# Linear attention of the second layer: weighted sums with the values stationary, denominators by running sums

## The chip, the cores and the metric

The kernel runs on one core of a Trainium2 chip. Its time is the device time of one execution in microseconds (us). TensorE (PE) multiplies, VectorE (DVE), ScalarE (ACT) and GpSimd (POOL) compute, SyncE (SP) only issues transfers. Every engine works through its own instructions in program order and waits on semaphores. Matrix products land in eight PSUM banks of 512 float32 columns; POOL cannot read them.

## The reference

Four layers follow each other on an input of 8 batches of 512 positions and 128 channels. Each layer adds an attention and a feed-forward part to its input. Only the attention of the second layer changes:

```
q = phi((x @ W_Q.T).reshape(b, t, H, DK))      # phi(u) = elu(u) + 1, H = 8 heads, DK = 64
k = phi((x @ W_K.T).reshape(b, t, H, DK))
v = (x @ W_V.T).reshape(b, t, H, DK)
gamma = sigmoid(decay_log)                     # one decay for each head
S = gamma * S + outer(k_t, v_t)                # for each position t
z = gamma * z + k_t
y_t = (S.T @ q_t) / (sum(z * q_t) + EPS)
gate = sigmoid(x @ W_g_w.T + W_g_b)
out = (y * gate) @ W_O.T
```

All of it is float32. The kernel does not run the recurrence for S: with scores a[s, t] = (k_s . q_t) * gamma^(t-s) for s <= t, the numerator is the sum over s of a[s, t] v_s, and the denominator is the sum over s of a[s, t].

## The kernel before, in words

Program text is written for each engine apart. In `layer1` the work of the 8 batches is cut into steps with a due time each (`of_batch`), in units of which one batch takes UNIT = 48. Each engine issues its steps in the order of due time plus a small delay for its kind (`LATER`); so the due times alone set how the steps of neighbouring batches are interleaved, and an engine that waits in one step holds up all behind it.

The steps of one batch of T = 512 positions (P = 128 rows, NT = 4 blocks of positions, FT = 4 blocks of two heads), in the order of a batch:

- The lead, 47 to 2 units ahead of the batch's own unit: `fetch` and `add_rows` (POOL issues 16 indirect transfers for the next batch, DVE adds the rows; this ends the layer before), `center`, `scale`, `norm` (PE transposes, L1588), `logit` (L1595), `rank` (L846 to L851), then eight `phi` (PE product of 512 columns L1606; ACT three passes L1543, L1544, L1546; POOL adds, L1499), four `gate` (L1611, ACT tanh L1556) and four `value` (L1616, ACT copy L1564). The products of the lead take turns in banks 0 and 1. `phi` n of ACT waits until POOL has done `phi` n-2. phi 0 to 3 are the keys, phi 4 to 7 the queries.
- The unit itself: for each pair of heads m = 0 to 3, three steps `decayed` on banks 4 to 7: PE makes the scores of two heads, 64 rows of the array each (L1630), DVE multiplies them by the table of decays (L1774).
- `weighted` (L1648), on banks 2 and 3, head by head: the decayed scores are the stationary operand, 128x128, and the values with a column of ones beside them (V1W = 65 columns) move. Ten products for each head, position on the output's partitions; column 64 is the denominator. PE issues each float32 product as two instructions.
- `divide`: DVE adds EPS, takes the reciprocal and multiplies (L1785 to L1787). `turn_y`: PE transposes y back to channels (L1659) and DVE multiplies by the gate (L1793).
- `out` (PE L1667, DVE L1800) is the product with W_O and the residual sum.

After the eight batches the routed feed-forward part of the layer follows; it waits for the last `out` (`attention_over`).

## Time and profile before

| | us |
|---|---|
| median of 3 runs | 2943.17 |
| lowest and highest | 2936.72, 2946.89 |
| the profiled execution | 2933.07 |
| its span in the trace | 2931.2 |
| start of this layer's own work to the first scores, 880 to 942.1 | 62.1 |
| first scores to the first `out`, 942.1 to 1018.91 | 76.8 |
| one batch, `out` to `out`, mean of the five from 1018.91 to 1308.37 | 57.9 |
| the last two batches | 51.4 and 39.2 |
| PE, DVE, ACT, POOL busy over the whole span | 84%, 53%, 45%, 20% |

A row of the windows view gives a stretch, its length, then each engine's busy time with its number of instructions, TensorE's granted clock as a share of full speed, the share of DMA and its rate. A row of a timeline gives start, duration, engine, line, operation, what it writes and reads, and in brackets how long the engine stood idle ahead of it and who released it. Neighbouring PE rows overlap by some 0.1 us at their ends, so the price of a group on a busy PE is read from start to start.

### The profile page before, as it was taken

The numbers are of one execution on the slowest core, as the hardware profiler recorded it, in microseconds if no ns is written. First come the engines' busy times: TensorE is split into PE (matmuls) and PEld (weight loads), VectorE is DVE, ScalarE is ACT, GpSimd is POOL, SyncE is SP. The second block draws the span as 40 slices with busy tenths as digits, with TensorE's granted clock in tenths as the row PEclk, the third lists the DMA queues.
The fourth block names the chain that finished last, engine by engine and source line by source line (L and its number), as shares of the span: only waits on it lengthen the run. The fifth ranks groups of instructions, "written<-read, shape, count | busy, mean of one in ns | idle before, by whom it ended". The sixth has DMA issues, their size and how long they took to land. (4 is left out here: it accounts for less than half of the span.)

```text
span 2931.2 us, 46008 instructions
## 1 busy us (share of the span) xinstructions
PE 2476.0 (84%) x16332; PEld 1580.8 (54%) x16466; DVE 1543.2 (53%) x3816; ACT 1325.9 (45%) x2462; POOL 589.7 (20%) x594
## 2 busy tenths in 40 slices
PE   3888887888884999999694788888877999999997
PEld 2455554787872666667693344444444555555553
DVE  6777775000013555654334666666636666666652
ACT  0455555444433333231131355555542666666665
POOL 3534331000006555441003111111001000000000
PEclk9999999999996899999896799999988999999999
DMA  3222221666661000000462211111112011111111
GB/s 113 90 87 73 78 85 43 185 196 190 199 179 57 23 25 26 19 19 4 127 187 79 71 44 52 54 53 49 46 42 66 28 44 50 50 50 41 32 34 30
DMA packets 117395, 214.10 MB, mean 73 GB/s; under 512 B 21000, under 2 KB 90160, under 8 KB 110256
## 3 DMA queue, kind: packets, MB, share of 16 engines
q1 hardware_dynamic: 104048, 186.88, 21.3%
q0 software_dynamic: 10240, 20.99, 2.5%
q10 hardware_dynamic: 2880, 3.28, 0.4%
q8 instruction: 133, 2.18, 0.3%
q14 instruction: 94, 0.77, 0.1%
HBM read 158.50 MB, written 51.40 MB: 72 GB/s over the span
## 5 line engine op out<-in xcount | busy, mean ns | idle before, releaser
L535 DVE TENSOR_REDUCE arena<-bank 128x1 f32<-128x512 f32 (+3 forms) x1216 | 775.7, 658 | 494.5 <-PE bank L525 246.7
L601 ACT ACTIVATE arena<-bank 128x512 f32<-128x512 f32 x640 | 373.3, 599 | 352.2 <-PE bank L591 347.6
L511 PE MATMUL bank<-arena 125*128 125x512 bf16 (+3 forms) x1536 | 460.2, 335 | 38.2 <-DMA arena<-q_parts 26.0
L601 ACT ACTIVATE arena<-bank,arena 128x512 f32<-128x512 f32 x512 | 337.3, 688 | 232.1 <-PE bank L586 73.0
L579 PE MATMUL bank<-arena 128*128 128x512 bf16 (+3 forms) x1402 | 389.2, 322 | 19.4 <-ACT arena L601 12.1
L616 PE MATMUL bank<-arena 128*32 128x512 f32 (+3 forms) x3072 | 315.8, 499 | 0.9 <-ACT arena L601 0.8
L579 PEld LDWEIGHTS bank<-arena 128*128 128x128 bf16 x1536 | 136.9, 99 | 248.6 <-ACT arena L601 140.1
L926 POOL DMA_INDIRECT back_rows<-sorted_out,back_now x160 | 154.3, 964 | 534.1 <-issue 256.2
L511 PEld LDWEIGHTS bank<-arena 125*128 125x128 bf16 x1536 | 139.7, 99 | 159.7 <-DVE arena L535 61.5
L1160 ACT ACTIVATE arena<-bank,arena 128x256 f32<-128x256 f32 x320 | 132.0, 470 | 195.4 <-PE bank L1210 195.4
L1306 DVE TENSOR_TENSOR arena<-bank,arena 128x256 f32<-128x256 f32 x80 | 33.9, 424 | 336.1 <-PE bank L1006 336.1
L1006 PE MATMUL bank<-arena 128*128 128x128 f32 x1664 | 202.5, 275 | 0.0
L1006 PEld LDWEIGHTS bank<-arena 128*128 128x128 f32 x1664 | 194.0, 192 | 0.1
L1210 PE MATMUL bank<-arena 128*128 128x256 f32 x640 | 159.1, 392 | 38.8 <-DMA arena<-in_L_ffn_w 38.6
L1774 DVE TENSOR_TENSOR arena<-bank,arena 128x512 f32<-128x512 f32 (+3 forms) x256 | 110.2, 482 | 149.5 <-PE bank L1630 149.5
L525 PE MATMUL bank<-mask_q,identb 128*128 128x128 bf16 (+2 forms) x704 | 176.1, 250 | 0.0
L1648 PEld LDWEIGHTS bank<-arena 128*128 128x128 f32 x1280 | 158.2, 200 | 31.7 <-issue 25.2
L591 PE MATMUL bank<-mask_k,identb 128*128 128x256 bf16 (+1 forms) x640 | 160.8, 251 | 12.2 <-DMA arena<-arena 8.0
L1648 PE MATMUL bank<-arena 128*128 128x65 f32 x1280 | 161.7, 284 | 3.7 <-DVE arena L1774 2.8
L1114 POOL DMA_INDIRECT sorted_in<-xn,arena x128 | 123.9, 968 | 154.9 <-PE bank L591 128.5
L1210 PEld LDWEIGHTS bank<-arena 128*128 128x128 f32 x640 | 117.1, 193 | 61.4 <-DMA arena<-in_L_ffn_w 47.9
L395 POOL TENSOR_SCALAR rstd<-mean_var 128x4 f32<-128x4 f32 x32 | 7.5, 236 | 702.0 <-DVE mean_var L367 618.2
(250 smaller groups left out, 3709.5 us busy)
## 6 DMA issues: line engine op xcount, KB each, us to landing
arena<-in_L_ffn_w SPq DMA_DIRECT2D x80, 578.0 KB, 4.0
arena<-k_parts SPq DMA_DIRECT2D x48, 576.0 KB
arena<-q_parts SPq DMA_DIRECT2D x48, 576.0 KB
arena<-in_L_ffn_w SPq DMA_DIRECT2D x24, 768.0 KB, 4.6
arena<-sorted_in SPq DMA_DIRECT2D x104, 128.0 KB, 2.4
sorted_out<-arena SPq DMA_DIRECT2D x104, 128.0 KB, 4.0
k_parts<-arena SPq DMA_DIRECT2D x24, 384.0 KB
q_parts<-arena SPq DMA_DIRECT2D x72, 128.0 KB
```

The lines of the kernel that those rows point to most:

```text
L511: ins = pe.matmul(mx[:, k * w:(k + 1) * w], Qx[0:KMAX, h, q * P:(q + 1) * P], Kx[0:KMAX, h, 0:w], start=(k == 0 or not L.causal), stop=not ...
L525: ins = pe.matmul(edge, identb[:], mask_q[:].unsqueeze(1).to_broadcast([P, n_heads, P]), start=False, stop=True, skip_group_check=True)
L535: dve.reduce_max(L.mx[:, g % 2, q, heads[0]:heads[-1] + 1], mx[:, 0:w * len(heads)].rearrange("p (j k) -> p j k", k=w), AX.X).then_inc(L.m ...
L579: ins = pe.matmul(st[:, c:c + w], Kx[:, h, kb * P:(kb + 1) * P], Qx[:, h, T - w:T], start=(c == 0), stop=not (L.causal or far), skip_group ...
L591: ins = pe.matmul(edge, identb[:], mask_k[:].unsqueeze(1).to_broadcast([P, len(at), P]), start=False, stop=True, skip_group_check=True)
L601: act.activation(L.probs[:, n % L.PR, 0:w], st[:, 0:w], ACT.Exp, scale=L.scale).then_inc(L.st_free.sem, 1)
L616: ins = pe.matmul(bank[2][j * VW:(j + 1) * VW, T - w:T], copy_of(L.Vx, b)[:, kb, g * HG + j, :], L.probs[:, (n + i) % L.PR, c:c + w], star ...
L926: pool.indirect_dma_start(back_rows[:, t, k, :], None, L.ys, bass.IndirectOffsetOnAxis(L.back_now[b.parity][:, r:r + 1], 0)).then_inc(L.go ...
L1006: ins = pe.matmul(bank[2 + j % 2][:, h * D:(h + 1) * D], L.hT[j % 2][:, f, h * P:(h + 1) * P], down(j, f), start=(f == 0), stop=(f == 3))
L1160: act.activation(L.hT[j % 2][:, c, :], bank[4 + n % 4][:, c % 2 * BLK:(c % 2 + 1) * BLK], ACT.Gelu, bias=L.wbuf[j % 3][:, L.B1 + c:L.B1 + ...
L1210: ins = pe.matmul(bank[4 + n % 4][:, c % 2 * BLK:(c % 2 + 1) * BLK], L.wbuf[j % 3][:, L.W1 + c * P:L.W1 + (c + 1) * P], L.xT[j % 2][:], st ...
L1648: ins = pe.matmul(bk[:, t * V1W:(t + 1) * V1W], L.am[:, SLOTS * (h % 4) + slot, c:c + P], L.V[b.parity][:, kb, h, :], start=(kb == 0), sto ...
```

## The change

The weighted sums are turned round: in `num` the values are stationary (64 columns for each head, so two heads lie side by side in the array, on output partitions 0 to 63 and 64 to 127 of one bank) and the decayed scores move (512, 384, 128 and 256 columns). The result has channels on partitions, so `turn_y` goes. The column of ones goes too; denominators are made in the lead instead:

- `prefix` m (DVE): a scan along the positions with gamma, from the keys of block m (this is z of the reference),
- `terms` m (POOL): z times the queries of block m,
- `den` (PE): four products with a small matrix `pick` sum the terms over the 64 channels of each head, into 8 rows of one bank; ACT copies them and adds EPS,
- `invert` (DVE): four reciprocals of 8x128,
- `wide` m (PE): a product with `spread` copies each head's row to its 64 partitions; DVE multiplies it into the gate.

In the unit DVE's `num` then multiplies bank by gate, and `divide` goes. `den` and `wide` take turns in banks 0 and 1 with the rest of the lead. Semaphores of other layers are shared through `tally` instead of being one each; the instructions of the other layers stay in their order.

```diff
             proj = [f"phi{n}" for n in range(2 * FT)] + [f"gate{c}" for c in range(FT)] + [f"value{t}" for t in range(NT)]
+            proj = proj[:10] + ["den"] + proj[10:] + [f"wide{m}" for m in range(FT)]
...
-            for m in range(H1 // 2):
-                head_names += [f"w{2 * m}", f"w{2 * m + 1}"] + ([f"yT{m - 1}"] if m else [])
-            head_names += [f"yT{FT - 1}", "out"]
+            head_names = [f"num{m}" for m in range(FT)] + ["out"]
...
-            LATER = {"dve": {"decayed": 0.8, "turn_y": 0.8, "out": 1.0, "logit": 0.8, "rank": 1.0},
-                     "act": {"norm": 0.7, "phi": 0.7, "gate": 0.7, "value": 0.7},
+            LATER = {"dve": {"decayed": 0.8, "num": 2.4, "out": 1.0, "logit": 0.8, "rank": 1.0, "wide": 1.0},
+                     "act": {"norm": 0.7, "phi": 0.7, "gate": 0.7, "value": 0.7, "den": 2.6},
...
+                k_at, q_at = (-38.0, -35.4, -32.8, -29.0), (-26.4, -23.8, -21.2, -18.6)
+                lead += [(at + 3.0, "prefix", m) for m, at in enumerate(k_at)]
+                lead += [(at + 2.9, "terms", m) for m, at in enumerate(q_at)]
+                lead += [(-13.0, "den", 0)] + [(-9.6 + 1.6 * t, "invert", t) for t in range(NT)]
+                lead += [(-1.2 + 1.7 * m, "wide", m) for m in range(FT)]
...
+                def terms(b, m):
+                    pool.wait_ge(L.phi.sem, L.phi.at(b, FT + m + 1))
+                    pool.wait_ge(L.summed.sem, L.summed.at(b, m + 1))
+                    settle(pool)
+                    z = L.z[:, m, :]
+                    pool.tensor_tensor(z, z, L.kq[b.parity]["q"][:, m, :], ALU.mult).then_inc(L.terms.sem, 1)
...
+                def den(b, _):
+                    bk = there(act, L, b, "den")
+                    if b.index:
+                        there(act, L, whole(b.index - 1), f"wide{FT - 1}")
+                    emptied(L, "den", act.activation(L.den[:], bk[0:H1, :], ACT.Identity, bias=L.eps[0:H1, 0:1]))
...
-                    for t in range(NT):
-                        for kb in range(t + 1):
-                            slot, c = where[kb]
-                            c += (t - kb) * P
-                            ins = pe.matmul(bk[:, t * V1W:(t + 1) * V1W],
-                                            L.am[:, SLOTS * (h % 4) + slot, c:c + P], L.V[b.parity][:, kb, h, :],
-                                            start=(kb == 0), stop=(kb == t))
...
+                    for kb, slot, c in [(0, 0, 0), (1, 1, 0), (3, 1, T - P), (2, 2, 0)]:
+                        for hh in range(2):
+                            h = 2 * m + hh
+                            ins = pe.matmul(bk[DK1 * hh:DK1 * (hh + 1), kb * P:T], L.V[b.parity][:, kb, h, :],
+                                            L.am[:, SLOTS * (h % 4) + slot, c:c + T - kb * P],
+                                            start=(kb == 0), stop=(kb == 2), skip_group_check=True)
+                    fill(L, f"num{m}", ins)
+
+                def den(b, _):
+                    bk = take(pe, L, b, "den")
+                    pe.wait_ge(L.terms.sem, L.terms.at(b, FT))
+                    for m in range(FT):
+                        ins = pe.matmul(bk[0:H1, :], L.pick[:, m * H1:(m + 1) * H1], L.z[:, m, :],
+                                        start=(m == 0), stop=(m == FT - 1))
+                    fill(L, "den", ins)
+
+                def wide(b, m):
+                    bk = take(pe, L, b, f"wide{m}")
+                    if m == 0:
+                        pe.wait_ge(L.inverse.sem, L.inverse.at(b, NT))
+                    fill(L, f"wide{m}", pe.matmul(bk[:], L.spread[:, m, :], L.den[:], start=True, stop=True))
...
+                def prefix(b, m):
+                    dve.wait_ge(L.phi.sem, L.phi.at(b, m + 1))
+                    there_before(dve, b, "den", 1)
+                    dve.tensor_tensor_scan(L.z[:, m, :], L.gamma[:, m:m + 1].to_broadcast([P, T]),
+                                           L.kq[b.parity]["k"][:, m, :], 0.0, ALU.mult, ALU.add
+                                           ).then_inc(L.summed.sem, 1)
+
+                def invert(b, t):
+                    ready(dve, L, b, "den")
+                    cols = slice(t * P, (t + 1) * P)
+                    dve.reciprocal(L.den[:, cols], L.den[:, cols]).then_inc(L.inverse.sem, 1)
+
+                def wide(b, m):
+                    bk = there(dve, L, b, f"wide{m}")
+                    ready(dve, L, b, f"gate{m}")
+                    th = L.th[b.parity][:, m, :]
+                    emptied(L, f"wide{m}", dve.scalar_tensor_tensor(out=th, in0=th, scalar=1.0, in1=bk[:], op0=ALU.add,
+                                                                    op1=ALU.mult))
+
+                def num(b, m):
+                    bk = there(dve, L, b, f"num{m}")
+                    ready(dve, L, b, f"wide{m}")
+                    if m == 0:
+                        there_before(dve, b, "out", 1)
+                    settle(dve)
+                    emptied(L, f"num{m}", dve.tensor_tensor(L.yT[:, m, :], bk[:], L.th[b.parity][:, m, :], ALU.mult))
```

Two places show the new order. The first is PE in the lead of batch 2, from its last `phi` to its third `gate`, before:

```order
L1606 MATMUL bank0<-xnT2,arena 128x512
L1648 MATMUL bank3<-arena 128x65 x10
L1630 MATMUL bank4<-arena 128x256
L1630 MATMUL bank5<-arena 128x256
L1611 MATMUL bank1<-xnT2,arena 128x512
L1611 MATMUL bank0<-xnT2,arena 128x512
L1659 MATMUL bank2<-ident,arena 128x128 x4
L1630 MATMUL bank6<-arena 128x512
L1630 MATMUL bank7<-arena 128x512
L1611 MATMUL bank1<-xnT2,arena 128x512
```

and now, where L1632 is `phi`, L1637 `gate`, L1656 the scores and L1682 `den`:

```order
L1632 MATMUL bank0<-xnT2,arena 128x512
L1656 MATMUL bank6<-arena 128x256
L1656 MATMUL bank7<-arena 128x256
L1637 MATMUL bank1<-xnT2,arena 128x512
L1637 MATMUL bank0<-xnT2,arena 128x512
L1682 MATMUL bank1<-arena 8x512 x4
L1656 MATMUL bank6<-arena 128x512
L1656 MATMUL bank7<-arena 128x512
L1637 MATMUL bank0<-xnT2,arena 128x512
```

The ten products of `weighted` and the transposes have left this stretch, and `den` stands two gates behind the last `phi`. The second place is POOL in a steady lead, from phi 3 to the scatter of the sorted rows (L926 and L925 are fetches, L1499 and L1506 `phi`, L1533 `terms`), before:

```order
L1499 TENSOR_TENSOR arena<-arena 128x512
L926 DMA back_rows<-sorted_out0,back_now0_1 128x128 x2
L1499 TENSOR_TENSOR arena<-arena 128x512
L926 DMA back_rows<-sorted_out0,back_now0_1 128x128 x2
L1499 TENSOR_TENSOR arena<-arena 128x512
L926 DMA back_rows<-sorted_out0,back_now0_1 128x128 x2
L1499 TENSOR_TENSOR arena<-arena 128x512 x2
L1512 DMA sorted_in1<-arena 36864x128 x4
```

and now, from phi 4 on:

```order
L1506 TENSOR_TENSOR arena<-arena 128x512
L925 DMA back_rows<-sorted_out0,back_now0_1 128x128
L1533 TENSOR_TENSOR arena<-arena 128x512
L925 DMA back_rows<-sorted_out0,back_now0_1 128x128
L1506 TENSOR_TENSOR arena<-arena 128x512
L925 DMA back_rows<-sorted_out0,back_now0_1 128x128
L1533 TENSOR_TENSOR arena<-arena 128x512
L925 DMA back_rows<-sorted_out0,back_now0_1 128x128
L1506 TENSOR_TENSOR arena<-arena 128x512
L1533 TENSOR_TENSOR arena<-arena 128x512
L1506 TENSOR_TENSOR arena<-arena 128x512
L1533 TENSOR_TENSOR arena<-arena 128x512
```

The four `terms` have come in between the last four `phi` and behind them, with the same fetches spread out singly.

## Rows read from the trace of the kernel before

**Rows 1.** The page: busy time, share of the span, instructions.
```profile
PE 2476.0 (84%) x16332; PEld 1580.8 (54%) x16466; DVE 1543.2 (53%) x3816; ACT 1325.9 (45%) x2462; POOL 589.7 (20%) x594
```

**Rows 2.** Windows: fill, first unit, batches 1, 2, 6 and 7 (out to out).
```profile
880.00:942.10 62.10, 27.49 (x60) 11.60 (x60) 14.15 (x62) 28.20 (x47) 40.98 (x42) 0.60 0.20 59
942.10:1018.91 76.81, 66.29 (x335) 43.25 (x334) 47.83 (x171) 22.23 (x39) 38.14 (x38) 0.84 0.08 23
1018.91:1075.41 56.50, 53.76 (x334) 36.93 (x333) 32.79 (x117) 19.46 (x34) 30.68 (x31) 1.00 0.09 24
1075.41:1135.48 60.07, 58.52 (x333) 39.56 (x333) 32.35 (x116) 19.04 (x34) 30.79 (x30) 0.91 0.09 23
...
1308.37:1359.80 51.43, 51.27 (x319) 35.43 (x319) 23.60 (x69) 17.16 (x30) 13.73 (x12) 1.00 0.02 6
1359.80:1398.96 39.16, 36.90 (x253) 30.76 (x253) 19.05 (x53) 0.00 (x0) 0.00 (x0) 0.87 0.01 1
```

**Rows 3.** Timeline of PE in a steady batch.
```profile
1193.71 3.84 PE L1667 MATMUL bank<-arena 128*128 128x128 f32 x32
1197.39 1.02 PE L1606 MATMUL bank<-xnT,arena 128*128 128x512 f32 x2
...
1202.69 0.41 PE L846 MATMUL bank<-arena,before_m 128*128 128x32 f32 x2
...
1204.50 2.73 PE L1648 MATMUL bank<-arena 128*128 128x65 f32 x20
1207.03 2.02 PE L1606 MATMUL bank<-xnT,arena 128*128 128x512 f32 x2
...
1215.29 1.08 PE L1606 MATMUL bank<-xnT,arena 128*128 128x512 f32 x2
1216.29 1.14 PE L1630 MATMUL bank<-arena 64*128 64x384 f32 x8
1217.36 1.12 PE L1606 MATMUL bank<-xnT,arena 128*128 128x512 f32 x2
1218.32 2.34 PE L1648 MATMUL bank<-arena 128*128 128x65 f32 x20
1220.60 0.70 PE L1630 MATMUL bank<-arena 64*128 64x256 f32 x4
1221.23 1.98 PE L1611 MATMUL bank<-xnT,arena 128*128 128x512 f32 x4
```

**Rows 4.** Timeline of POOL in the same batch: phi 1, phi 3, a fetch, phi 6 and 7.
```profile
1200.28 1.27 POOL L1499 TENSOR_TENSOR arena<-arena 128x512 f32<-128x512 f32 x1 [2.16 <-ACT arena L1546]
...
1210.91 1.27 POOL L1499 TENSOR_TENSOR arena<-arena 128x512 f32<-128x512 f32 x1 [2.10 <-ACT arena L1546]
...
1217.26 0.94 POOL L926 DMA_INDIRECT back_rows<-sorted_out,back_now  x1 [0.31 <-issue]
...
1221.89 2.50 POOL L1499 TENSOR_TENSOR arena<-arena 128x512 f32<-128x512 f32 x2
```

**Rows 5.** Timelines of PE, then of its weight loads, third layer: four heads side by side.
```profile
2699.41 1.07 PE L616 MATMUL bank<-arena 128*32 128x512 f32 x8
2700.41 0.39 PE L579 MATMUL bank<-arena 128*128 128x512 bf16 x1
...
2699.41 0.16 PEld L616 LDWEIGHTS bank<-arena 128*32 128x32 f32 x8
```

**Rows 6.** Groups by shape: busy, mean ns | idle before them. Gate product, reciprocals.
```profile
L1793 DVE SCALAR_TENSOR_TENSOR arena<-arena,bank 128x512 f32<-128x512 f32 x32 | 21.2, 681 | 10.6 <-PE bank L1659 10.6
...
L636 DVE RECIPROCAL arena<-bank 128x16 f32<-128x16 f32 x96 | 23.8, 248 | 36.3 <-PE bank L630 36.3
...
L1786 DVE RECIPROCAL arena<-arena 128x4 f32<-128x4 f32 x64 | 11.4, 178 | 2.2
```

**Rows 7.** Timeline of POOL in the fill, batch 0: phi 4 and phi 7.
```profile
929.58 1.27 POOL L1499 TENSOR_TENSOR arena<-arena 128x512 f32<-128x512 f32 x1
...
938.05 1.27 POOL L1499 TENSOR_TENSOR arena<-arena 128x512 f32<-128x512 f32 x1
```

More of the change, by code:

```diff
@@ L1333, in layer1 @@
             L.relu, L.neg = [L.phi_work[:, i * 2 * T:(i + 1) * 2 * T].rearrange("p (i t) -> p i t", i=2) for i in range(2)]
-            L.V = [carve([P, NT, H1, V1W]) for _ in range(2)]
+            L.V = [carve([P, NT, H1, DK1]) for _ in range(2)]
+            L.gamma, L.eps = carve([P, FT]), carve([P, 1])
+            L.pick, L.spread = carve([P, FT * H1]), carve([H1, FT, P])
+            L.den = carve([H1, T])
             L.th = [carve([P, FT, T]) for _ in range(2)]
@@ L1353, in layer1 @@
             last = used[0]
[L1356 removed]
+            L.dist = L.z[:, 0, :]
             used[0] = here
@@ L1439, in of_batch @@
                     steps += [(12.0 * m + 4.0 * i, "decayed", (m, i)) for i in range(SLOTS)]
-                    steps += [(weigh + 2.0, "weighted", 2 * m), (weigh + 4.9, "divide", 2 * m),
-                              (weigh + 5.6, "weighted", 2 * m + 1), (weigh + 8.2, "divide", 2 * m + 1)]
-                steps += [(at, "turn_y", c) for c, at in enumerate((34.5, 46.5, UNIT + 8.9, UNIT + 9.9))]
-                steps.append((UNIT + 12.2, "out", 0))
+                    steps.append((weigh + 1.5, "num", m))
+                steps.append((UNIT + 7.0, "out", 0))
                 return steps
@@ L1534, in act_prog @@
                                    scale=L.lng[:, h:h + 1]).then_inc(L.decay_act, 1)
+                for h in range(H1):
+                    rows = slice(DK1 * (h % 2), DK1 * (h % 2 + 1))
+                    act.activation(L.gamma[rows, h // 2:h // 2 + 1], L.lng[rows, h:h + 1],
+                                   ACT.Exp).then_inc(L.decay_act, 1)
                 def norm(b, _):
@@ L1653, in turn_y @@
-                def turn_y(b, c):
-                    bk = take(pe, L, b, f"yT{c}")
-                    for h in (2 * c, 2 * c + 1):
-                        if turns(L, f"w{h}").bank is not bk:
-                            ready(pe, L, b, f"w{h}")
-                    for t in range(NT):
-                        ins = pe.transpose(bk[:, t * P:(t + 1) * P], L.y[:, t, c * P:(c + 1) * P], ident[:])
-                    fill(L, f"yT{c}", ins)
+                    for h in (2 * m, 2 * m + 1):
+                        for i in (1, 2):
+                            ready(pe, L, b, f"s{h}.{i}")
@@ L1670, in pe_prog @@
                 each_trip(pe, {"norm": norm, "logit": logit, "rank": rank, "phi": phi, "gate": gate, "value": value,
-                               "decayed": decayed, "weighted": weighted, "turn_y": turn_y, "out": project}, LATER["pe"])
+                               "decayed": decayed, "num": num, "den": den, "wide": wide, "out": project}, LATER["pe"])
                 attention_over(pe)
@@ L1777, in decayed @@
                         emptied(L, f"s{h}.{i}", ins)
-                def divide(b, h):
-                    bk = there(dve, L, b, f"w{h}")
-                    if h % 2 == 0 and turns(L, f"yT{h // 2}").bank is not bk:
-                        there_before(dve, b, f"yT{h // 2}", 1)
-                    num = bk[:, 0:NT * V1W].rearrange("p (t c) -> p t c", t=NT)
-                    cols = slice(h * DK1, (h + 1) * DK1)
-                    link(dve, L, dve.tensor_scalar(L.den[:], num[:, :, DK1], EPS1, 2.0, ALU.add, ALU.mult))
-                    link(dve, L, dve.reciprocal(L.rec[:], L.den[:]))
-                    emptied(L, f"w{h}", dve.tensor_tensor(L.y[:, :, cols], num[:, :, 0:DK1],
-                                                          L.rec[:].unsqueeze(2).to_broadcast([P, NT, DK1]), ALU.mult))
@@ L1807, in dve_prog @@
                 each_trip(dve, {"decay": decay, "locate": locate, "add_rows": add_rows, "center": center, "scale": scale, "logit": logit, "rank": rank, "decayed": decayed,
-                                "divide": divide,
-                                "turn_y": turn_y, "out": residual}, LATER["dve"])
+                                "prefix": prefix, "invert": invert, "wide": wide, "num": num, "out": residual}, LATER["dve"])
                 attention_over(dve)
```

120 lines of the change are left out of this document (59 added, 61 removed).

## The prediction

> **What bounds the kernel now.** Over the whole span PE is busy 84% and no other engine over 53% [rows 1], but that is an average over layers that the change leaves alone. So I read the windows of this layer's attention first. Between the first `out` and the sixth a batch takes 56.5 to 60.1 us, and PE is busy in all but 1.5 to 2.7 us of it, DVE for 32 to 33, POOL for 31, ACT for 19 [rows 2]. Steady batches are PE's. The fill in front is not: there PE works 27 of 62 us at a granted clock of 0.60, and POOL is busy for 41 [rows 2]. The batch at clock 1.00 takes 56.5 us, its neighbour at 0.91 takes 60.1 [rows 2]; a 512-column product that goes from start to start in 1.0 us takes 1.9 in a slow stretch (1215.29 to 1216.29, and 1207.03 with its 2.02 [rows 3]). The mean of the five steady batches is (1308.37 - 1018.91) / 5 = 57.9 us.
>
> Next I read POOL in a steady batch. From its phi 3 at 1210.91 to the end of phi 7 at 1224.39 it hardly rests: five additions of 1.27 and six fetches of some 0.95 + 0.3 make 13.5 us [rows 4]. PE is not held up by that, since nothing that it issues soon needs phi 7: it starts its own phi 7 at 1217.36 and goes on to gates and weighted sums [rows 3] while POOL finishes 7 us later. The next to need all phi are the scores of the following batch, some 25 us on. The change puts a reader right into this gap.
>
> **PE's work, part by part.** Gone: `weighted`, 80 products a batch. A head goes from start to start in 2.2 to 2.5 us (1218.32 to 1220.60, 1204.50 to 1207.03 [rows 3]); at 2.2 for most, 8 make 17.8. Gone: four `turn_y` of four transposes, at an eighth of `out`'s 3.7 us (1193.71 to 1197.39 for 32 instructions, four of which are 0.5 [rows 3]): 2.1. Added: `den` and `wide`, four products of 512 columns each, 1.0 apiece: 4 + 4. Whether eight rows or 128 are used of the array makes no difference to the columns that stream, and I take the full price.
>
> Added: `num`, for a pair of heads 512 + 384 + 128 + 256 = 1280 columns. If the two heads run side by side, the price of a pair is that of one: the scores, which share the array by rows, take 1.07 for both heads' 384 + 128 (1216.29 to 1217.36 [rows 3]), and by columns the third layer runs four heads of 512 columns, eight instructions, in 1.00 us [rows 5]. So 1280 / 512 x 1.06 = 2.65 a pair, 10.6 a batch; if they ran in turn it would be 21.2. I take 10.6, by the row with the same arrangement.
>
> The Trainium skill ("TensorE: Matmul & The Clock Gate", part 3, the mechanism) says that a weight load overlaps running products only where its row group differs. Both heads use all rows here, so by that rule the loads of `num` would stand open. The trace disagrees: eight loads over one row group took no time beside the 1.00 us of their products [rows 5].
>
> So PE's own work changes by 10.6 + 4 + 4 - 17.8 - 2.1 = -1.3 us a batch. The idle 2.7 us at the turn to `out` [rows 2], where PE waited for `divide` and the gates, partly go: `num` needs one DVE product of 0.68 (as the gate's [rows 6]) before `out`. I keep 1.6 of the 2.7 for waits on DVE's `wide`, on the inverses and on the input of the next batch. PE alone would then need 56.5 - 1.3 - 1.1 = 54.1 us at full clock.
>
> **The new wait, the largest term.** `den` waits for the fourth `terms`, and behind it in PE's order stand all other work: scores, two gates, `num`, values. How late is it? From the start of phi 3, PE has up to `den`: phi 3 to 7 and two gates at 1.0, scores of 0.64, 1.06, 1.07 and 0.64 (1220.60 to 1221.23, 1216.29 to 1217.36 [rows 3]), one `num` of 2.65: 13.1 us. POOL can begin phi 3 when PE's product is done and ACT's three passes: 1197.39 to 1200.28, 2.9 after the start on PE [rows 3, 4]. It then needs the 13.5 of before and four `terms`, each the same 128x512 operation, 1.27: 18.6. Also, POOL comes to phi 3 late: from phi 0 on it has three additions and seven fetches, some 12.2 us, where PE has three phi, scores of 1.06 and 1.07, one `num` and the ranks (1202.69 to 1204.50 [rows 3]), 9.6: 2.5 late. So `den` starts at 2.9 + 2.5 + 18.6 = 24.0 after phi 3 instead of 13.1: PE stands 10.9 us, part of it before gate 1 (whose bank ACT frees after POOL's phi 5), 6 or 7 right before `den`. Bounds: if POOL were not late and its fetches fell in its gaps, 6; if scans or reciprocals held POOL or DVE up, 13. POOL does not catch up, because the fetches come in order with the rest, and each batch repeats it.
>
> After such a pause the clock: in the fill, with its pauses, 0.60 is granted, and in the slow rows 1.9 replaces 1.0 [rows 2, 3]. Four products of `den` at 1.9 cost 3.5 more (bounds 0 and 6, if the following products are slow as well). Steady batch: 54.1 + 10.9 + 3.5 = 68.5; against 57.9, **+10.6, five times: +53**.
>
> **DVE** loses `divide` and the gate products. The gates alone are 4 x 0.68, and `num` and `wide` add eight such [rows 6]. Reciprocals: 16 columns take 248 ns, 4 take 178 [rows 6], 5.8 ns a column; 128 columns then take 0.9, four pieces 3.6 us. Four scans of 512 have no row; between a product of that size, 0.68, and three times it: 2.7 to 8 us, and I take 4.5. With the removed 8.8 (8 x 0.76 for `divide`, 2.7 for gates) the 32.5 busy us [rows 2] become some 37 of 68: beside PE's. But a scan waits for POOL's phi, with the decayed scores behind it on DVE; by the same walk that holds `num` 1 up 1 us, in front of a PE that waits at `den` anyway.
>
> **The fill.** POOL is busy from phi 4 at 929.58 to the end of phi 7 at 939.32 [rows 7], and the scores began at 942.1. Now `terms` 0 to 3 join (+5.1) and one more fetch (+1.3): T3 ends at 945.7. `den` at the slow rate 7.6, two gates and four values 6, one `wide` 1: first scores at about 960, +18 (at full clock +14.5). I take **+17**. The eight small exponentials and the copy for `spread` at the start hide in ACT's and DVE's idle time, POOL's short memsets likewise: 0.
>
> **First unit** (76.8 us [rows 2]): it was stretched by waits for batch 1's rows, which POOL now delivers ahead of the later scores, so about 8 us of it go and the 10.6 come: **+2.5** (bounds -5 and +8). **Sixth interval** (51.4 [rows 2]): the lead of batch 7 has no fetches, so POOL is done with T3 2 us after PE: -1.3 - 1.1 + 2 and a slow product or two, **+2**. **Last interval** (39.2 [rows 2]): no lead, so only 10.6 - 17.8 - 2.1 = -9.3, and most of 2.3 us waits and a clock of 0.87: **-12**.
>
> **Sum** 17 + 2.5 + 53 + 2 - 12 = +62.5. The profiled execution took 2933.1, which gives 2995.6; it lies 10 under the median of the runs, 2943.2, so the forecast for a median is 2943.2 + 62.5, near 3005.
>
> **Rivals.** *PE's work decides* and POOL's chain stays hidden, because POOL runs ahead of my walk or the fetches thin out: steady -2.6 x 5, fill +15, first unit -8, last two -12: near 2925. For it: PE's sum is smaller, and POOL is busy for only 31 of 58 us. Against: these 31 us come in one piece, where `den` reads. 13%. *Half of the stall*: POOL not late, clock kept: 5 x 4 instead of 53, near 2972. 12%. *The side-by-side heads don't overlap*: 10.6 more a batch, of which 2.65 fall into the stall, 8 x 8 on top: near 3069. Against it are the four heads [rows 5]. 7%. *Nothing moves*, gains and stall cancel: 4%, near 2943. The other 64% is the forecast.
>
> The rival that ends faster decides from the point where T3 ends before PE reaches `den`; by the walk 10.9 us are missing.
>
> **Chances and range.** About 0.3% is what a measurement of this kernel can tell from no change. Faster by more: the first rival, 13%. Within: 4%. Slower: 83%. The forecast's own bounds are 2975 to 3035; downward I go on to 2960 to take in the halved stall, upward to 3070 for heads that don't overlap; 17% is left out below.
>
> **What would show it.** PE's rows of `den` with an idle time of 6 to 7 us released by POOL's `terms` in batches 1 to 6, and about 2 in batch 7; `num` at 2.6 to 2.7 us a pair; `out` to `out` 66 to 70 us; first scores near 960; the last interval near 27. If `den` starts without a wait, the largest term falls; if `num` takes 5.3 a pair, the heads don't overlap.

## The result and the profile after

The changed kernel takes 3040.5 us in the median of four runs (3032.7 to 3050.0), the kernel before beside it 2943.7 (2936.7 to 2946.9): a ratio of 1.034, 95% interval 1.0305 to 1.0377. It is slower by 97 us. The forecast was 3005; the time lies 35 us above it, 5 above the 3035 that the forecast gave as its own upper bound, and inside the stated range of 2960 to 3070. The profiled execution took 3050.0, 10 above the median, where that of before lay 10 below; so the two traces differ by 117 us, not 97. 109 of them lie between the start of this layer and its last `out` (the table below); the rest of the kernel behind it takes 1540.0 us against 1532.2, and what makes that, no run shows.

First the page, busy time of each engine, to be held against [rows 1], and the same windows as [rows 2]: the fill, the first unit, batches 1 and 2, batches 6 and 7 (busy time of each engine, then the granted clock).

```profile
PE 2500.3 (82%) x15698; PEld 1470.3 (48%) x15698; DVE 1582.2 (52%) x3721; ACT 1331.1 (44%) x2478; POOL 657.1 (22%) x628
```

```profile
880.00:965.58 85.58, 33.18 (x70) 13.03 (x70) 21.66 (x71) 30.80 (x57) 53.85 (x50) 0.61 0.18 55
965.58:1059.78 94.20, 71.89 (x228) 28.50 (x228) 50.34 (x140) 19.79 (x35) 40.95 (x36) 0.72 0.05 14
1059.78:1132.17 72.39, 58.17 (x237) 24.79 (x237) 36.37 (x104) 19.95 (x35) 39.55 (x34) 0.84 0.07 19
1132.17:1206.93 74.76, 59.17 (x239) 24.05 (x238) 37.41 (x106) 19.94 (x35) 39.53 (x34) 0.84 0.07 18
...
1425.24:1481.52 56.28, 52.27 (x235) 22.43 (x233) 29.51 (x71) 20.02 (x35) 19.35 (x16) 0.97 0.02 5
1481.52:1508.20 26.68, 21.45 (x151) 12.01 (x149) 16.27 (x36) 0.00 (x0) 0.00 (x0) 1.00 0.01 2
```

The whole-span shares hardly moved. The windows did:

| stretch | before [rows 2] | after | difference | forecast |
|---|---|---|---|---|
| fill, up to the first scores | to 942.1 | to 965.6 | +23.5 | +17 |
| first unit | 76.8 | 94.2 | +17.4 | +2.5 |
| a steady batch, mean of five | 57.9 | 73.1 | +15.2 (x5 = +76) | +10.6 (x5 = +53) |
| sixth interval | 51.4 | 56.3 | +4.9 | +2 |
| last interval | 39.2 | 26.7 | -12.5 | -12 |
| sum | | | +109 | +62.5 |

Of the fill's 23.5 us, 1.8 are there before its first product on PE (909.24 against 907.47). In batch 2 (1132.17 to 1206.93) PE is busy for 59.2 of 74.8 us, where a batch of before was busy in all but 1.5 to 2.7. The rest is waiting. Here is PE in that batch (start, duration, operation; in brackets the idle time before it and who ended it):

```profile
1146.77 1.10 PE L1632 MATMUL bank<-xnT,arena 128*128 128x512 f32 x2
1147.81 0.70 PE L1656 MATMUL bank<-arena 64*128 64x256 f32 x4
1154.28 2.07 PE L1632 MATMUL bank<-xnT,arena 128*128 128x512 f32 x2 [5.77 <-DVE gates L1796]
1156.28 1.85 PE L1656 MATMUL bank<-arena 64*128 64x512 f32 x4
...
1159.12 2.37 PE L1673 MATMUL bank<-arena 128*64 128x512 f32 x16
1161.42 1.13 PE L1632 MATMUL bank<-xnT,arena 128*128 128x512 f32 x2
...
1168.12 1.12 PE L1637 MATMUL bank<-xnT,arena 128*128 128x512 f32 x2 [1.76 <-ACT arena L1563]
1176.03 6.38 PE L1682 MATMUL bank<-arena 128*8 128x512 f32 x8 [6.79 <-POOL arena L1533]
...
1195.13 1.94 PE L1656 MATMUL bank<-arena 64*128 64x512 f32 x4
1197.00 2.07 PE L1690 MATMUL bank<-arena 8*128 8x512 f32 x2
1199.00 3.92 PE L1673 MATMUL bank<-arena 128*64 128x512 f32 x16
```

L1682 is `den`: it waits 6.79 us for POOL's fourth `terms` (L1533), as forecast. But 22 us earlier phi 4 (L1632 at 1154.28) waits 5.77 us for DVE's last step of the ranks (L1796), a wait that the prediction does not have. The numerator of a pair of heads, L1673, takes 2.30 us from start to start (1159.12 to 1161.42), and 3.84 in the slow stretch near the batch's end.

POOL and DVE in the same stretch. L925 is a fetch (its first word is the start), L1506 phi, L1533 `terms`, L1816 the scan.

```profile
1141.19 1.29 POOL L1506 TENSOR_TENSOR arena<-arena 128x512 f32<-128x512 f32 x1
1142.65 1.87 POOL L925 DMA_INDIRECT back_rows<-sorted_out,back_now  x1 [0.16 <-issue]
1144.82 0.94 POOL L925 DMA_INDIRECT back_rows<-sorted_out,back_now  x1 [0.30 <-issue]
...
1156.17 1.27 POOL L1506 TENSOR_TENSOR arena<-arena 128x512 f32<-128x512 f32 x1
1157.60 1.87 POOL L925 DMA_INDIRECT back_rows<-sorted_out,back_now  x1 [0.16 <-issue]
...
1174.62 1.26 POOL L1533 TENSOR_TENSOR arena<-arena 128x512 f32<-128x512 f32 x1 [0.20 <-POOL arena L1506]
```

```profile
1142.52 1.23 DVE L1816 TENSOR_TENSOR_SCAN arena<-arena 128x512 f32<-128x512 f32 x1 [1.65 <-POOL arena L1506]
...
1151.66 1.23 DVE L1816 TENSOR_TENSOR_SCAN arena<-arena 128x512 f32<-128x512 f32 x1 [1.44 <-POOL arena L1506]
1152.81 0.17 DVE L858 TENSOR_TENSOR arena<-bank,arena 128x32 f32<-128x32 f32 x1
...
1154.05 0.18 DVE L1796 RECIPROCAL gates<-arena 128x4 f32<-128x4 f32 x1
1154.14 0.72 DVE L1808 TENSOR_TENSOR arena<-bank,arena 128x256 f32<-128x256 f32 x2
1157.48 1.23 DVE L1816 TENSOR_TENSOR_SCAN arena<-arena 128x512 f32<-128x512 f32 x1 [2.61 <-POOL arena L1506]
```

Two things are to be seen. The ranks' steps (L858 to L1796) stand on DVE behind the third scan, and that scan waits for POOL's phi 2. And a fetch that is issued while a scan runs takes 1.87 us instead of 0.94, four times a batch; the others of this batch take 0.94 to 1.11, as the fetch of [rows 4] did.

### The profile page after: what moved, and what is told of

Read it like the earlier page. It is cut to its first block and busy times, and to the rows that moved or that the text cites. A ratio compares the mean times of both kernels' runs of the same rounds, so it can differ in the third digit from the quotient of the medians.

```text
span 3048.2 us, 44632 instructions
## 1 busy us (share of the span) xinstructions
PE 2500.3 (82%) x15698; PEld 1470.3 (48%) x15698; DVE 1582.2 (52%) x3721; ACT 1331.1 (44%) x2478; POOL 657.1 (22%) x628
## 5 line engine op out<-in xcount | busy, mean ns | idle before, releaser
L578 PE MATMUL bank<-arena 128*128 128x512 bf16 (+3 forms) x1536 | 440.8, 328 | 26.8 <-ACT arena L600 12.4
L925 POOL DMA_INDIRECT back_rows<-sorted_out,back_now x160 | 180.4, 1127 | 543.7 <-issue 299.1
L1005 PEld LDWEIGHTS bank<-arena 128*128 128x128 f32 x1664 | 194.4, 192 | 0.1
L1209 PEld LDWEIGHTS bank<-arena 128*128 128x128 f32 x640 | 117.8, 194 | 61.6 <-DMA arena<-in_L_ffn_w 47.8
L1632 PE MATMUL bank<-xnT,arena 128*128 128x512 f32 x128 | 84.2, 756 | 43.8 <-DVE gates L1796 43.8
L615 PEld LDWEIGHTS bank<-arena 128*32 128x32 f32 x3072 | 67.2, 108 | 103.6 <-issue 60.6
```

The source lines that it names most:

```text
L578: ins = pe.matmul(st[:, c:c + w], Kx[:, h, kb * P:(kb + 1) * P], Qx[:, h, T - w:T], start=(c == 0), stop=not (L.causal or far), skip_group ...
L615: ins = pe.matmul(bank[2][j * VW:(j + 1) * VW, T - w:T], copy_of(L.Vx, b)[:, kb, g * HG + j, :], L.probs[:, (n + i) % L.PR, c:c + w], star ...
L925: pool.indirect_dma_start(back_rows[:, t, k, :], None, L.ys, bass.IndirectOffsetOnAxis(L.back_now[b.parity][:, r:r + 1], 0)).then_inc(L.go ...
L1005: ins = pe.matmul(bank[2 + j % 2][:, h * D:(h + 1) * D], L.hT[j % 2][:, f, h * P:(h + 1) * P], down(j, f), start=(f == 0), stop=(f == 3))
L1209: ins = pe.matmul(bank[4 + n % 4][:, c % 2 * BLK:(c % 2 + 1) * BLK], L.wbuf[j % 3][:, L.W1 + c * P:L.W1 + (c + 1) * P], L.xT[j % 2][:], st ...
```

## The experiments

In all of them the base is the changed kernel unless said otherwise. "Rank wait" is PE's idle time at phi 4, "`den` wait" that before `den`. The first four kernels ran beside each other (kernel before: 2933.8 us there), the next four beside each other on another chip (kernel before: 3044.7 there), the last two on a third one (2940.3 and 2941.5). On the second chip the four traces show the first scores of this layer at 1045.7 to 1066.8 us, all the others at 939.5 to 965.6, so runs of different chips are compared by ratio and by the length of a batch alone. Behind each kernel stands its ratio to the kernel before, with its 95% interval; the changed kernel has 1.034 (1.0305 to 1.0377) and batches of 71.7 to 74.9 us, 73.1 in the mean of five.

**1. Ranks ahead of the scans.** Is the wait that I had missed a cost of its own?

```diff
-                lead += [(at + 3.0, "prefix", m) for m, at in enumerate(k_at)]
+                lead += [(at, "prefix", m) for m, at in enumerate((-29.1, -28.2, -27.3, -25.4))]
```

> The changed kernel, but VectorE's four scans of a lead have later due times, so that the ranks of the router come ahead of them in its order. In the changed kernel PE stands 5.8 us before phi 4, until VectorE's last instruction on the ranks frees bank 1, and 6.8 us before den. Theory (GpSimd's chain of fetches, phi and terms ends last, 38 us from its first fetch to its fourth terms, and the 5.8 us lie inside it): the wait before phi 4 goes, the wait before den grows by as much, the time stays within 10 us of 3040. Rival (both waits add up on PE): 5 to 6 batches x 5.8 us and some slow clock, about 3005 or less.

Measured: 3036.9 us, 1.035 of before (1.031 to 1.040). PE in a steady batch:

```profile
1211.55 1.12 PE L1632 MATMUL bank<-xnT,arena 128*128 128x512 f32 x2 [1.70 <-DVE gates L1796]
...
1227.69 2.08 PE L1637 MATMUL bank<-xnT,arena 128*128 128x512 f32 x2 [3.73 <-ACT arena L1563]
1235.61 5.23 PE L1682 MATMUL bank<-arena 128*8 128x512 f32 x8 [5.84 <-POOL arena L1533]
```

The rank wait falls from 5.77 to 1.70 us, and the ratio shows no gain. The wait before `den` did not grow, as the theory had it (5.84 after 6.79); two us more stand at a gate (3.73 instead of 1.76), some 2 more in pieces of 0.9 to 1.0. In the one trace of each kernel the batches take 70.0 to 71.7, 71.1 in the mean, 2.0 under the changed kernel's; the fourth and fifth take the same 71.7 in both, and the sixth interval takes 3.4 more here. So the greater part of the 4.1 us taken from the rank wait comes back at other places: PE runs toward a `den` that POOL releases when it can, and a wait ahead of it is part of the same lateness and not simply added to it.

**2. Short scans.** Eight of 512 positions are scanned; the other prefix sums are left out, all waits stay.

```diff
-                    dve.tensor_tensor_scan(L.z[:, m, :], L.gamma[:, m:m + 1].to_broadcast([P, T]),
-                                           L.kq[b.parity]["k"][:, m, :], 0.0, ALU.mult, ALU.add
+                    dve.tensor_tensor_scan(L.z[:, m, 0:8], L.gamma[:, m:m + 1].to_broadcast([P, 8]),
+                                           L.kq[b.parity]["k"][:, m, 0:8], 0.0, ALU.mult, ALU.add
```

> The changed kernel with scans over 8 positions instead of 512; the running sums of the other positions are left out, every instruction keeps its place. In the changed kernel the first fetch behind each of phi 0 to 3 takes 1.87 us on GpSimd instead of 0.95, while a scan of 1.23 us runs on VectorE. Theory (the scan holds up the fetch, and that lengthens the chain that den waits for): all fetches at about 0.95, the chain 3.7 us shorter, 6 batches x 3.7 = 22 us less, about 3018. Rival (fetches are slow for another reason, or the chain does not decide): fetches stay at 1.87, or the time stays near 3040.

Measured: 3011.5 us, 1.026 (1.023 to 1.030): 25 us less than run 1 beside it, and by the ratios some 23 less than the changed kernel, as the theory had it. A steady batch takes 69.0 us in the mean of five, 4.1 less than in the changed kernel. The same line of the view of one source in three kernels (shortest, median and longest fetch in ns): before, after, short scans.

```profile
L926 POOL DMA_INDIRECT back_rows<-sorted_out,back_now x160: 940/947/1107, 877.3 to 2042.1; - x160
```

```profile
L925 POOL DMA_INDIRECT back_rows<-sorted_out,back_now x160: 940/954/1931, 879.1 to 2155.3; - x160
```

```profile
L925 POOL DMA_INDIRECT back_rows<-sorted_out,back_now x160: 940/954/1106, 872.9 to 2121.9; - x160
```

With the scans goes every fetch above 1.11 us. DVE was not short of time there; in batch 2 of the changed kernel it stands for 17.41 us around `den`:

```profile
1183.50 0.69 DVE L1808 TENSOR_TENSOR arena<-bank,arena 128x512 f32<-128x512 f32 x1 [17.41 <-PE bank L1656]
```

So what came back came through POOL: four fetches are 3.7 us shorter. The rank wait falls with them, from 5.77 to 2.9, while the wait before `den` stays at 6.6 to 6.8.

**3. `den` later.** `den` moves from behind gate 1 to behind the values, with the reciprocals and `wide` after it:

```diff
-            proj = proj[:10] + ["den"] + proj[10:] + [f"wide{m}" for m in range(FT)]
+            proj = proj + ["den"] + [f"wide{m}" for m in range(FT)]
...
-                lead += [(-13.0, "den", 0)] + [(-9.6 + 1.6 * t, "invert", t) for t in range(NT)]
-                lead += [(-1.2 + 1.7 * m, "wide", m) for m in range(FT)]
+                lead += [(-2.2, "den", 0)] + [(-0.4 + 0.2 * t, "invert", t) for t in range(NT)]
+                lead += [(1.6 + 1.3 * m, "wide", m) for m in range(FT)]
```

> The changed kernel with den due at -2.2 instead of -13 (behind the last value instead of between two gates), the inverses and wide behind it. Theory (where den stands in PE's order makes the 6.8 us wait and the slow clock after it): the wait before den goes in batches 2 to 6, the 5.8 us before phi 4 stay, out to out about 64 instead of 73 us, the fill 5 us shorter, about 2980. Rival (the array work added is what costs: den, wide and num themselves): no more than 10 us under 3040.

Measured: 2991.3 us, 1.020 (1.017 to 1.023), batches of 64.1 to 66.0.

```profile
1132.17 2.08 PE L1632 MATMUL bank<-xnT,arena 128*128 128x512 f32 x2 [5.78 <-DVE gates L1796]
...
1158.07 3.60 PE L1682 MATMUL bank<-arena 128*8 128x512 f32 x8
```

A batch takes 65.2 in the mean, where the theory had about 64 (and 2980 in all). `den` has no wait, and its four products take 3.60 us instead of 6.38, with no pause right ahead of them. That is the largest term of the prediction, shown: the place of `den` costs 42 of the 97 us (the ratios 1.034 and 1.020). The rank wait of 5.78 stays.

**4. Numerators alone.** Everything about the denominators is left out: scans, `terms`, `den`, reciprocals, `wide` and the product with them in the gate.

> One part of the change alone: num with the values stationary; scans, terms, den, inverses and wide are left out, so the denominators are not divided out and the gate lacks its + 1. Theory (num takes 2.31 us a pair against 4.5 for two heads of weighted, and transposes and divide are gone): out to out 45 to 48 us instead of 57.9 of the kernel before, last interval 27, in all 80 to 95 us less than before, about 2855. Rival (heads side by side or the mixed order cost something else, such as drains between kinds of tiles): out to out above 52, over 2900.

Measured: 2876.5 us, 0.981 (0.978 to 0.984). A steady batch takes 52.2 us on average, the first unit 62.2. The gain is real (57 us) but smaller than the 80 to 95 of the theory, whose batches were to take 45 to 48; they lie just over the rival's bound of 52, the whole lies under its 2900. PE's work did shrink, and waits for others stand beside it. In the window of a steady batch PE is busy for 45.4 of 51.0, and the waits in the batch just ahead of it, which is as long, are these:

```profile
1211.85:1262.84 50.99, 45.37 (x223) 21.18 (x222) 29.23 (x94) 19.39 (x34) 30.86 (x30) 0.97 0.10 27
```

```profile
1178.89 1.62 PE L1632 MATMUL bank<-xnT,arena 128*128 128x512 f32 x2 [1.71 <-DVE gates L1796]
1191.98 1.13 PE L1637 MATMUL bank<-xnT,arena 128*128 128x512 f32 x2 [1.08 <-ACT arena L1563]
1211.38 0.63 PE L1614 MATMUL bank<-ident,arena 128*128 128x128 f32 x4 [2.84 <-DVE arena L1761]
```

So of the two halves of the change the numerators give back 5.7 us a batch, and the denominators cost 73.1 - 52.2 = 20.9.

**5. Both moves.** Runs 1 and 3 together.

> den late and the ranks ahead of the scans, together. Late den alone gave 65.3 us from out to out, with 5.8 us of waiting before phi 4; ranks first alone gave 71.7 against 71.7. Theory (with den out of the way of GpSimd's chain, the wait for the ranks is what is late next): now the early ranks do pay, 5 to 6 us a batch, out to out 59 to 60 us, about 2955. Rival (GpSimd's chain still ends last, through the waits of phi on each other): out to out 64 or more, no less than 2980.

Measured: 3100.4 us, 1.020 (1.016 to 1.024), batches of 65.0 to 67.7, no better than run 3 alone.

```profile
1226.80 1.13 PE L1632 MATMUL bank<-xnT,arena 128*128 128x512 f32 x2 [1.69 <-issue]
...
1242.94 2.08 PE L1637 MATMUL bank<-xnT,arena 128*128 128x512 f32 x2 [3.73 <-ACT arena L1563]
```

My theory fell: I had taken the rank wait for one that can be had once `den` is away. The rival is what came: POOL's chain is still last. ACT waits for POOL's phi and PE for ACT, so what left phi 4 stands at the gate, 3.73 us.

**6. Fetches earlier.** From batch 3 on, the fetches begin at -96 with a gap of 1.1 instead of -88 and 1.3, into POOL's idle time ahead of phi 0; `den` and ranks stay as changed. (`locate` moves from -90 to -97 likewise.)

```diff
-                    begin, gap = (-89.0, 1.6) if second else (-82.0, 1.15) if n == 2 else (-88.0, 1.3)
+                    begin, gap = (-89.0, 1.6) if second else (-82.0, 1.15) if n == 2 else (-96.0, 1.1)
```

> The changed kernel with GpSimd's sixteen fetches of batches 3 to 7 due 8 units earlier and closer together (and the step that locates the rows with them), den where the change put it. Theory (the length of GpSimd's chain from its first fetch to its fourth terms sets when den starts): 8 to 9 us of fetches lie ahead of phi 0, the wait before den shrinks from 6.8 to under 1 us in batches 3 to 6 as far as the wait for the ranks leaves it, out to out near 66 instead of 72 to 75, about 3015. Rival (the four terms and their order behind the last phi decide alone, whatever the fetches do): out to out over 71, 3035 or more.

Measured: 3127.8 us, 1.030 (1.025 to 1.034), batches of 66.2 to 71.6.

```profile
1255.18 2.07 PE L1632 MATMUL bank<-xnT,arena 128*128 128x512 f32 x2 [8.69 <-DVE gates L1796]
1271.05 3.59 PE L1682 MATMUL bank<-arena 128*8 128x512 f32 x8 [2.78 <-POOL arena L1533]
```

Batches take 68.5 in the mean, 4.6 under the changed kernel's, where the theory had 66; the two ratios' intervals overlap, so for the whole kernel a gain isn't clear. The `den` wait shrinks from 6.8 to 2.8, not to under 1, and now the rank wait is real: 8.69. POOL does phi 2 and 3 in a row and then has nothing to do for 6.4 us, because PE itself holds phi 4 back:

```profile
1259.12 1.27 POOL L1506 TENSOR_TENSOR arena<-arena 128x512 f32<-128x512 f32 x1 [6.42 <-ACT arena L1565]
```

In the changed kernel the two waits were one lateness; here they no longer are.

**7. All three.** Runs 1, 3 and 6 together.

> den late, ranks first and fetches early in one kernel. If GpSimd's chain is nobody's last input any more once den is late, early fetches bring nothing over the two others together: the same within 8 us. If phi 4 to 7 still wait for fetches, 2 to 4 us a batch less, about 2935.

Measured: 3072.6 us, 1.012 (1.008 to 1.016), batches of 60.9 to 61.4. Against run 5, from which it differs by the fetches alone, that is 4.9 us a batch, more than the 2 to 4 of the expectation, so phi 4 to 7 did still wait for fetches. The 2935 that stood beside it (a ratio of 1.00) is missed all the same: it was counted down from the 2955 that run 5 did not reach. In run 6, with the ranks behind the scans, the same fetches brought 4.6 us a batch.

**8. `den` packed.** On top of run 7, the four products of `den` stand side by side in four groups of 32 columns, and `wide` reads them from four groups of 32 rows in pairs (`pick`, `spread` and the copy of `den` are laid out to match):

```diff
-                        ins = pe.matmul(bk[0:H1, :], L.pick[:, m * H1:(m + 1) * H1], L.z[:, m, :],
-                                        start=(m == 0), stop=(m == FT - 1))
+                        ins = pe.matmul(bk[32 * m:32 * (m + 1), :], L.pick[:], L.z[:, m, :], start=True, stop=True,
+                                        skip_group_check=True)
...
-                    fill(L, f"wide{m}", pe.matmul(bk[:], L.spread[:, m, :], L.den[:], start=True, stop=True))
+                    fill(L, f"wide{m}", pe.matmul(bk[:], L.spread[32 * m:32 * (m + 1), :], L.den[32 * m:32 * (m + 1), :], start=True, stop=True))
```

> The kernel with all three orders changed, and den and wide packed: den's four products lie side by side in the array (32 columns each, 32 rows of the bank for each block of heads), wide's products use 32 rows of the array each and run two at a time on banks 0 and 1. Theory (side by side products cost the time of one, as num's): den takes 1.1 instead of 4.1 us, a pair of wide 1.1 instead of 2.1, PE has 5 us a batch less, 35 to 40 us less in all than the same order without packing, near 2900. Rival (such small tiles run one after another, or PE is not what is late): under 10 us less.

Measured: 3052.4 us in nine runs, 1.003 (1.001 to 1.005), batches of 59.0 to 60.9.

```profile
1272.13 4.53 PE L1673 MATMUL bank<-arena 128*64 128x512 f32 x16 [3.11 <-DVE arena L1810]
...
1294.01 1.06 PE L1682 MATMUL bank<-arena 128*32 128x512 f32 x8
...
1301.05 1.28 PE L1690 MATMUL bank<-arena 32*128 32x512 f32 x4 [2.62 <-DVE arena L1825]
```

`den` takes 1.06 us instead of 3.60: the prediction's "I take the full price" was right for the layout of the change and is not a property of the sum. The gain, 20 us, is under the 35 to 40 that I expected, and a steady batch gains only 1.3 of its 5: PE's waits rise from 4.0 us a batch in run 7 to between 6.8 and 9.2. DVE is late at two places: the decayed scores behind three scans (3.10 in run 7 already), and now `wide` behind four reciprocals in a row (2.62 instead of 0.91).

**9. DVE's work spread.** Scans, `terms`, `den` and reciprocals set apart from each other:

```diff
-                lead += [(at, "prefix", m) for m, at in enumerate((-29.1, -28.2, -27.3, -25.4))]
-                lead += [(at + 2.9, "terms", m) for m, at in enumerate(q_at)]
-                lead += [(-2.2, "den", 0)] + [(-0.4 + 0.2 * t, "invert", t) for t in range(NT)]
+                lead += [(at, "prefix", m) for m, at in enumerate((-29.1, -25.1, -21.3, -17.5))]
+                lead += [(at, "terms", m) for m, at in enumerate((-22.6, -20.0, -16.6, -13.0))]
+                lead += [(-9.0, "den", 0)] + [(-6.6 + 1.6 * t, "invert", t) for t in range(NT)]
```

> The packed kernel with its vector work spread: the keys' scans at -29.1, -25.1, -21.3 and -17.5 of their batch instead of -29.1 to -25.4, the terms at -22.6, -20.0, -16.6 and -13.0, the small product behind the gates (-9.0) and its four reciprocals at -6.6 to -1.8 instead of back to back behind it. The packed kernel still lost in a batch of 60 us: 3.1 at numerator 1 (VectorE's decayed scores behind three scans), 2.6 at the first wide product (3.4 us of reciprocals in a row), 1.0 to 1.5 at the transposed input. Theory (these waits are VectorE work that stands too thick, not too much of it): they go, a batch takes 55 to 57 us, the whole is 12 to 22 us below the packed kernel, 0.990 to 0.996 of the kernel before, so the change's idea beats the kernel before when each wait is taken from it. Rival (VectorE or GpSimd is as full as the matrix engine, and a wait only moves): 59 to 60 us a batch and within 0.3% of the packed kernel's 1.003, with the waits on other releasers.

Measured: 2930.5 us in twelve runs against 2940.3, 0.996 (0.994 to 0.998), 0.7% or 20 us under run 8 by the ratios. Batches take 55.6 to 58.5, 57.3 in the mean of five, 2.7 under run 8's 60.0: the theory's direction and its whole, a little over its 55 to 57 a batch. Three waits over 1 us were left:

```profile
1191.43 2.37 PE L1673 MATMUL bank<-arena 128*64 128x512 f32 x16 [2.08 <-DVE arena L1810]
...
1197.89 2.67 PE L1690 MATMUL bank<-arena 32*128 32x512 f32 x4 [1.97 <-DVE arena L1831]
1202.46 1.12 PE L1614 MATMUL bank<-ident,arena 128*128 128x128 f32 x4 [1.90 <-DVE arena L1831]
```

**10. Reciprocals and `wide` earlier.** On top of run 9:

```diff
-            LATER = {"dve": {"decayed": 0.8, "num": 2.4, "out": 1.0, "logit": 0.8, "rank": 1.0, "wide": 1.0},
+            LATER = {"dve": {"decayed": 0.8, "num": 2.4, "out": 1.0, "logit": 0.8, "rank": 1.0, "wide": 0.2},
...
-                lead += [(-9.0, "den", 0)] + [(-6.6 + 1.6 * t, "invert", t) for t in range(NT)]
-                lead += [(2.0 + 2.6 * (m // 2) + 0.05 * m, "wide", m) for m in range(FT)]
+                lead += [(-9.0, "den", 0)] + [(at, "invert", t) for t, at in enumerate((-7.6, -7.5, -6.0, -4.6))]
+                lead += [(0.7 + 1.3 * (m // 2) + 0.02 * m, "wide", m) for m in range(FT)]
```

> The spread kernel with three numbers moved: the reciprocals at -7.6, -7.5, -6.0 and -4.6 (the first two into VectorE's 2.5 us of idleness at 1182.2 of the spread kernel's trace), the wide products at 0.7 and 2.0 instead of 2.0 and 4.6, VectorE's readings of them 0.2 behind instead of 1.0. The spread kernel takes 58.2 us a batch; its matrix engine waits 2.08 at numerator 3 (decayed scores behind reciprocals), 1.97 at the second pair of wide products and 1.90 at the next batch's transposes (both until VectorE has read wide products), 5.9 in all, beside 52 of work. Theory: these are places and not amounts of VectorE work, so 3.5 to 5.9 us a batch go: 52.5 to 55 us, the whole 20 to 33 us lower, 0.985 to 0.990 of the kernel before. Rival: VectorE is full there (1186 to 1203 without a gap), so the wait returns at another place: 57 to 59 us a batch and 0.994 to 0.998 of the kernel before.

Measured: 2912.1 us against 2941.5, 0.989 (0.987 to 0.991): the fastest full kernel of this study, 29 us under the kernel before and, by the ratios, 4.4% under the changed one. Batches take 52.2 to 54.6, 53.9 in the mean, as the theory had it. The window of a steady batch, and the two waits that are left in it besides two of 0.5:

```profile
1146.18:1200.68 54.50, 50.67 (x238) 23.57 (x237) 41.96 (x105) 19.96 (x35) 38.30 (x34) 0.94 0.09 25
```

```profile
1174.35 1.12 PE L1637 MATMUL bank<-xnT,arena 128*128 128x512 f32 x2 [0.87 <-ACT arena L1563]
...
1194.64 2.67 PE L1690 MATMUL bank<-arena 32*128 32x512 f32 x4 [2.01 <-DVE arena L1831]
```

## Why the prediction came out as it did

**The mechanism was right.** `den` stands where POOL has just fallen behind, PE waits 6.79 us there (forecast 6 to 7), 2.77 in batch 7 (forecast about 2), and run 3 shows that its place is what costs. The heads of a numerator do run side by side: 2.30 us a pair, under the forecast 2.65. The last interval, where no lead exists, fell by 12.5 (forecast 12). The slower case had to be the likely one. By its number alone the rival of heads that don't overlap, 3069, lies nearer to the measured 3040 than the forecast of 3005 does; the 2.30 us a pair rule it out. And the range held by luck in part: its stretch above 3035 was put there for that rival, and what filled it were other things, told below. (In the first rival a steady batch is reckoned with -2.6; the prediction's own terms give -1.3 - 1.1 = -2.4, which moves its 2925 by 1 us.)

**The size of a steady batch was off by 4.6 us** in the mean of five (73.1 against 68.5). Batch 2, one of the two longest, is off by 6.3 and can be split by the prediction's own sum:

| term | forecast | measured |
|---|---|---|
| PE's work at full clock | 52.5 | 51.5 |
| waits at the turn to `out` | 1.6 | 1.3 (0.70 and 0.57) |
| lateness of POOL's chain | 10.9 | 14.3 (5.77 + 1.76 + 6.79) |
| slow clock | 3.5 | 7.7 |
| sum | 68.5 | 74.8 |

*The chain.* From phi 3 on PE (1146.77) to `den` (1176.03) it takes 29.3 us where I had walked 24.0. Of the three pieces 2.9 + 2.5 + 18.6 the middle one failed: POOL came to phi 3 at 1156.17, 6.5 us late and not 2.5, because three of the fetches ahead of it took 0.93 longer beside a scan (2.8 in all) and its phi 0 began 3.8 after PE's own and not 2.9 (1137.39 on PE, 1141.19 on POOL); the rest is rounding and a PE that was 0.2 quicker. The third was 19.7, with one more such fetch. I had priced the scan for DVE (4.5 us; it is 4.9) and said that it costs PE nothing there. That was true, and I did not ask what it does to POOL. The rank wait of 5.77 was missed as well, but in run 1 most of it goes and the ratio stays: it is for the greater part a place where the same lateness stands.

*The clock.* I let it fall for `den` alone. With two pauses it falls twice and once more at the end of the batch: from start to start `den` took 2.7 us more than at full rate, phi 4 and the scores behind it 1.7, scores, one `wide` and a numerator from 1195.13 to 1202.84 together 3.3. The mean granted clock is 0.84 in these batches against 0.91 to 1.00 in [rows 2]. In run 3, whose longest pause is the rank wait, `den` ran at full rate. In batches 4 and 5 PE waits as long as in batch 2 (15.4 us), but its busy time is 56.3 us at a granted clock of 0.88 instead of 59.2 at 0.84, and they take 71.7: the same pauses cost unlike amounts of clock. No run takes the clock's share out by itself, so its 7.7 us are read from rows and not tried.

**The fill**: T3 was forecast to end at 945.7 and `den` began at 951.25, 5.5 us later. From POOL's phi 4 (935.05) on, its chain took the 16.1 us of the forecast; ahead of it stand four fetches beside scans, of 1.86 to 1.93 us (+3.7), and the 1.8 by which the layer began later. From `den` to the scores it is 14.3, as forecast. With the short scans the scores began 10.6 us earlier than in the changed kernel, 6.0 of which are there at the layer's first product already.

**The first unit** is the step that failed by most, +17.4 against +2.5. I took 8 us off for waits that the changed order would remove. They did not go: PE stands for 22.3 of the 94.2 us (5.11 at the ranks, 5.88 at `den`, 4.8 at the first numerator and the next input, the rest in pieces under 2.1), and at a clock of 0.72 (0.84 before) its work takes 5.6 us more than before. That the denominators make it is shown by run 4, in which the first unit takes 62.2; how much of it is waiting and how much clock is not told apart. I had credited a gain without a row that carried it.

The medians moved by 12 us less than the sum of the intervals, and by 20 less than the two traces. These are single executions, one at the low and one at the high end of its kernel's runs, which hold a difference of that size; no run here tells more of it.

The Trainium skill ("TensorE: Matmul & The Clock Gate", part 3, the mechanism) lets a weight load overlap running products only where its row group differs; the same section also names a background weight buffer, which no run here can show. The numerators settle what the prediction left to another layer's row: sixteen loads over all 128 rows stand in 2.30 us for 1280 columns, so the trace disagrees with the rule of the row group for two column groups.

## What to carry to other kernels

A reader put into a long chain of another engine's work costs what that engine is late by at that place, and the waits ahead of it can be the same lateness: find the chain's own end, and move the reader behind it, before mending any single wait. After each move look again which engine is late; here removing one of several waits changed no ratio twice (runs 1 and 5), while removing them in turn and packing the small products made a loss of 3.4% into a gain of 1.1%. When DVE gets an instruction with two inputs from SBUF, price what it does to GpSimd's instructions beside it as well as its own time, and where several small products share one bank, see whether column groups let them run at once.

## What the hardware showed that was not expected

- The issue of an indirect DMA by GpSimd takes 0.94 us alone and 1.87 beside a DVE scan of 1.23 us, and returns to at most 1.11 when the scans are cut to eight positions. It goes the other way too: in runs 9 and 10, where two additions of POOL run beside it, one scan a batch takes 3.8 us instead of 1.2 (the 32 scans have a mean of 1769 ns in run 10, 1225 in the changed kernel); two rows of run 9 stand below. The Trainium skill ("SBUF — State Buffer", Who interferes with whom) says that a DVE instruction with two SBUF inputs and a GpSimd instruction that reads SBUF hold one shared pair of ports in turn, and that the other fully blocks; the trace agrees in both directions: where no long scan runs (the kernel before and run 2), no fetch takes over 1.11 us. That the issue of a fetch is such an instruction is taken from these times.

```profile
1165.33 3.80 DVE L1818 TENSOR_TENSOR_SCAN arena<-arena 128x512 f32<-128x512 f32 x1
...
1165.54 2.49 POOL L1506 TENSOR_TENSOR arena<-arena 128x512 f32<-128x512 f32 x2
```

- A reciprocal over 128 columns takes 918 ns in the mean on eight rows (the changed kernel) and 919 on 128 (run 10), against 178 over four columns [rows 6]: the columns cost, not the rows.
- The scan over 512 columns takes 1225 ns where a product of that size takes 681 [rows 6].
- Four products of 512 columns with 32 columns of weights each take 1.06 us in column groups and 3.60 one after the other into the same rows; in the slow stretch of the changed kernel they took 6.38.
